# Opening the second layer's attention inside the first feed-forward's last batch, and selection logits two batches ahead

## The reference, cut to what matters

```python
xn = layernorm(x)
x = x + L0_attn(xn) + L0_ffn(xn)      # causal attention, 16 heads of 16; FFN: silu(w1 x)*(w2 x), gelu(h1 .), gelu(h2 .), w3, ternary weights 256/1024
xn = layernorm(x)
x = x + L1_attn(xn) + L1_ffn(xn)
# L1_attn: softmax(q k^T / 4 + pos_bias[h, i, j]) v, then Wout
# L1_ffn, in groups of 16 tokens, for 64 expert slots:
logits = grouped @ controller + tie
perm = logits == max(logits over the 16 tokens)
sel = perm^T grouped;  inter = relu(sel @ f1 + bias) @ f2;  out = perm inter
```

## Time and profile before

| | us |
|---|---|
| median of 3 runs | 2090.08 |
| lowest, highest | 2089.43, 2093.64 |
| the profiled execution's own time | 2090.87 |
| its span, first to last instruction | 2089.0 |
| PE busy over the span | 1777.4 (85%) |
| DVE busy | 1168.1 (56%) |
| ACT busy | 1057.0 (51%) |
| POOL busy | 984.3 (47%) |
| mean granted TensorE clock | 0.931 |

### The profile page before, as it was taken

One profiled execution on the slowest core, in us unless ns is written; L12 is line 12 of the kernel. 1 busy time (PEld: TensorE's weight loads), 2 busy tenths in 40 slices (PEclk: granted clock), 3 DMA queues, 4 the chain that ended last, 5 costly groups with the idle time before them and its releaser, 6 DMA issues. The chain is left out here.

```text
span 2089.0 us, 34151 instructions
## 1 busy us (share of the span) xinstructions
PE 1777.4 (85%) x11015; PEld 1144.5 (55%) x11015; DVE 1168.1 (56%) x2538; ACT 1057.0 (51%) x1439; POOL 984.3 (47%) x736
## 2 busy tenths in 40 slices
PE   4888898887999999999997848878878888866999
PEld 2455555544878788788785623334334334334566
DVE  5666666562243353353442348877877877926535
ACT  1555555555422232232222117877877877963542
POOL 3344444432333434334333317776776776954202
PEclk7999999997999999999998958989989989988999
DMA  3333333315411120111110173232222222107346
GB/s 109 93 102 101 97 91 101 86 47 177 143 61 33 45 78 23 55 53 43 60 43 24 34 258 87 62 77 85 61 73 89 61 71 81 32 11 289 100 150 212
DMA packets 119221, 182.52 MB, mean 87 GB/s; under 512 B 14197, under 2 KB 73077, under 8 KB 119146
## 3 DMA queue, kind: packets, MB, share of 16 engines
q1 hardware_dynamic: 109214, 170.45, 27.1%
q10 hardware_dynamic: 9296, 9.05, 1.3%
q0 software_dynamic: 640, 2.10, 0.3%
HBM read 90.72 MB, written 39.91 MB: 63 GB/s over the span
## 5 line engine op out<-in xcount | busy, mean ns | idle before, releaser
L803 POOL TENSOR_TENSOR l_prob<-l_prob,l_bias 128x1024 f32<-128x1024 f32 x192 | 452.2, 2377 | 148.4 <-ACT l_prob L918 147.6
L1202 POOL TENSOR_TENSOR f_hl<-f_full,f_hh 128x512 fp32r<-128x512 f32 x192 | 247.6, 1290 | 425.6 <-DVE f_hh L1240 271.2
L985 DVE CUSTOM_DVE_ANT_0 l_slot<-l_slot,l_bias 128x512 f32<-128x512 f32 x512 | 340.8, 716 | 52.0 <-PE l_slot L1063 51.0
L921 ACT ACTIVATE l_prob<-l_prob 128x1024 f32<-128x1024 f32 x256 | 271.1, 1071 | 0.0
L472 DVE TENSOR_REDUCE l_peak<-l_slot 128x2 f32<-128x256 f32 (+3 forms) x256 | 206.4, 822 | 108.1 <-PE l_slot L564 105.8
L1288 PE MATMUL f_ps<-f_hh,f_hi_h 128*128 128x512 f32 x1024 | 259.9, 391 | 0.8 <-ACT f_attn L1168 0.4
L1288 PE MATMUL f_ps<-f_hl,f_hi_h 128*128 128x512 f32 x1024 | 258.4, 390 | 0.0
L388 ACT ACTIVATE l_prob<-l_slot 128x1024 f32<-128x1024 f32 (+3 forms) x256 | 174.8, 706 | 101.7 <-PE l_slot L583 99.3
L1288 PEld LDWEIGHTS f_ps<-f_hh,f_hi_h 128*128 128x128 f32 x1024 | 192.3, 188 | 43.3 <-ACT f_hh L1214 2.1
L1288 PEld LDWEIGHTS f_ps<-f_hl,f_hi_h 128*128 128x128 f32 x1024 | 192.4, 188 | 39.7
L918 ACT COPY l_prob<-l_slot 128x1024 f32<-128x1024 f32 x192 | 194.8, 1014 | 36.6 <-PE l_slot L1079 35.8
(11 more groups left out here) (205 smaller groups left out, 2844.4 us busy)
## 6 DMA issues: line engine op xcount, KB each, us to landing
l_stacks<-l_parts SPq DMA_DIRECT2D x384, 128.0 KB, 2.6
attn<-l_out_sb ACTq DMA_DIRECT2D x16, 512.0 KB, 2.9
f_raw<-in_L_ffn_h_w SPq DMA_DIRECT2D x16, 512.0 KB, 3.8
f_raw<-in_L_ffn_h_w SPq DMA_DIRECT2D x32, 256.0 KB, 2.6
e_w<-in_L_ffn_f SPq DMA_DIRECT2D x32, 256.0 KB, 2.9
l_bias<-ext SPq DMA_DIRECT2D x16, 448.0 KB, 6.4
l_x_in<-in_L_attn_x SPq DMA_DIRECT2D x8, 512.0 KB, 3.9
xh<-l_xh SPq DMA_DIRECT2D x8, 512.0 KB, 2.6
```

The source lines that it names most:

```text
L803: return eng.tensor_tensor(probs(n), src, bias[:, h:h + 2, j * P:j * P + T], ALU.add)
L921: act.activation(probs(n), probs(n), ACT.Exp).then_inc(p_exp.sem, 1)
L985: ins = dve.tensor_tensor_reduce(src, src, bias[:, 4 * g + 2 * pr + a, t * P:t * P + T], 1.0, 3 * NEG, ALU.add, ALU.max, peak[:, g, a, pr, ...
L1202: pool.tensor_tensor(t.hl[layer % 2][:, o], t.full[:, n % 2], t.hh[layer % 2][:, o].bitcast(F32), ALU.subtract).then_inc(self.h_lo.sem, 1)
```

## The change

1. `biased_attention` and `layers` become generators, so that the feed-forward's block can hold work of layer 1. The tiles are laid out anew so that what is written early in layer 1 lies on tiles that are dead by then; no tile's size or type changes.
2. In the last feed-forward batch the seven pieces are rounded and compared beside h1 instead of h2. The maxima are reduced behind h1, PE turns them behind h2's third tile, and DVE makes the flag beside the fourth.
3. The branch block is gone. Each engine reads the flag inside the feed-forward block (`if_not_exact`): SP after the last pieces are issued, POOL, ACT and PE behind their last batch, DVE between its last cast and the output.
4. Behind that the opening of layer 1 follows in the same block. SP: rows, constants, weights and twelve bias heads, then the store of the last output. POOL: the power, then both halves of `stacks`. ACT: four weights, four rows. DVE: statistics and shift ahead of the output, four weight remainders behind it.
5. The wait for the last store moves from the end of the feed-forward block to SP's load of batch 1's rows.
6. In layer 1's block stay POOL's fills (key row source, now 2x512 instead of 2x4096 and broadcast, and the ones) and the last four bias heads at once.
7. In selection SP, DVE and PE run by `two_ahead`: after PE's fourth product of batch b come the transposes of b + 1 and then the logits of b + 2. DVE makes the blocks of b + 1, then logits, maximum and mask of b + 2. All eight copies are ACT's. The experts' first loads are issued after the first logits' operands of batch 1 instead of before.

The core of the diff:

```diff
+        def load_bias(sp, g):
+            for h in range(4 * g, 4 * g + 4):
+                rising = bass.AP(w["ext"].tensor, w["ext"].offset + h * 2 * T, [[1, P], [1, UW]])
+                sp.dma_start(bias[:, h], rising).then_inc(bias_in[g].sem, 16)
+
+        def open_sp(sp):
+            sp.dma_start(x_in[:], x_d[0].rearrange("(t p) d -> p t d", p=P)).then_inc(x_loaded.sem, 16)
+            for dst, src in ((power, c["c_pow"]), (ident, c["c_ident"])):
+                sp.dma_start(dst[:], src).then_inc(consts_in.sem, 16)
+            for name, ap in w["loads"]:
+                for dst, src in w["place"](name, raw[name], ap):
+                    sp.dma_start(dst, src).then_inc(w_in[name].sem, 16)
+            sp.dma_start(raw["o"], w["wo"].rearrange("(k p) n -> p k n", p=P)).then_inc(w_in["o"].sem, 16)
+            for g in range(QUADS - 1):
+                load_bias(sp, g)
+
+        def open_pool(pool):
+            pool.wait_ge(consts_in.sem, 16 * 2)
+            pool.wait_ge(eps_done.sem, 1)
+            pool.tensor_tensor(rstd[:], var_eps[:], power[:], ALU.pow).then_inc(rstd_ready.sem, 1)
+            pool.memset(stacks[:, 0].bitcast(F32), 0.0).then_inc(blank.sem, 1)
+            pool.memset(stacks[:, 1].bitcast(F32), 0.0).then_inc(blank.sem, 1)
+
+        def open_act(act):
+            for name in names + ("o",):
+                act.wait_ge(w_in[name].sem, 16)
+                act.activation({"q": wq, "k": wk, "v": wv, "o": wo}[name][:, 0], raw[name], ACT.Copy,
+                               scale=HD ** -0.5 if name == "k" else 1.0).then_inc(w_high.sem, 1)
+            act.wait_ge(shift_ready.sem, 1)
+            for t in range(TT):
+                act.activation(xn[:, t], x_in[:, t], ACT.Identity, bias=shift[:, t:t + 1],
+                               scale=rstd[:, t:t + 1]).then_inc(xn_ready.sem, 1)
+
+        def open_dve(dve):
+            dve.wait_ge(x_loaded.sem, 16)
+            for t in range(TT):
+                dve.bn_stats(stats[:, t], x_in[:, t]).then_inc(stats_done.sem, 1)
+            for t in range(TT):
+                dve.wait_ge(stats_done.sem, t + 1)
+                dve.bn_aggr(moments[:, t], stats[:, t]).then_inc(moments_done.sem, 1)
+            dve.wait_ge(moments_done.sem, TT)
+            dve.tensor_scalar(var_eps[:], moments[:, :, 1], EPS, None, ALU.add).then_inc(eps_done.sem, 1)
+            dve.wait_ge(rstd_ready.sem, 1)
+            dve.scalar_tensor_tensor(shift[:], moments[:, :, 0], -1.0, rstd[:], ALU.mult, ALU.mult)\
+               .then_inc(shift_ready.sem, 1)
+
+        def open_weights(dve):
+            for m, (name, dst) in enumerate((("q", wq), ("k", wk), ("v", wv), ("o", wo))):
+                dve.wait_ge(w_high.sem, m + 1)
+                dve.scalar_tensor_tensor(dst[:, 1], raw[name], HD ** -0.5 if name == "k" else 1.0,
+                                         dst[:, 0].bitcast(F32), ALU.mult, ALU.subtract).then_inc(w_ready.sem, 1)
+
+        opening_of = Opening()
+        opening_of.sp, opening_of.pool, opening_of.act, opening_of.dve, opening_of.weights = \
+            open_sp, open_pool, open_act, open_dve, open_weights
+        yield opening_of
...
+                        if isinstance(b, int) and b == 1:
+                            sp.wait_ge(x_stored.sem, x_stored.at(1, B - 1))
...
-                        if n in (1, 2) and opening(b):
-                            load_bias(n + 1)
...
                 sp.wait_ge(blank.sem, 3)
-                sp.dma_start(stacks[HROWS - 1:P:HROWS, 1].bitcast(F32), minus).then_inc(keyed.sem, 16)
-                for g in range(2):
-                    load_bias(g)
+                sp.dma_start(stacks[HROWS - 1:P:HROWS, 1].bitcast(F32), minus.unsqueeze(1).to_broadcast([2, PAIRS, T])).then_inc(keyed.sem, 16)
+                load_bias(sp, QUADS - 1)
...
                 pool.memset(minus, -1.0).then_inc(blank.sem, 1)
-                pool.memset(stacks[:, 1].bitcast(F32), 0.0).then_inc(blank.sem, 1)
-                pool.wait_ge(consts_in.sem, 16 * 2)
+                pool.memset(vals_sb[:], 0.0).then_inc(ones_ready.sem, 1)
+                pool.wait_ge(ones_ready.sem, 1)
+                pool.memset(vals[:, :, HD:HD + 1], 1.0).then_inc(ones_ready.sem, 1)
...
-                dve.memset(vals_sb[:], 0.0).then_inc(ones_ready.sem, 1)
-                dve.wait_ge(ones_ready.sem, 1)
-                dve.memset(vals[:, :, HD:HD + 1], 1.0).then_inc(ones_ready.sem, 1)
-                dve.memset(stacks[:, 0].bitcast(F32), 0.0).then_inc(blank.sem, 1)
...
+        if rows_ahead:
+            rows_ahead()
...
+                if beside:
+                    beside(KH + n)
...
+    def if_not_exact(eng, again):
+        eng.wait_ge(found.sem, 3)
+        with eng.If(eng.value_load(flag[0:1, 0:1], min_val=0, max_val=1) == 1):
+            eng.sem_inc(idle.sem, 1)
+            eng.wait_ge(idle.sem, 5)
+            again(eng)
...
+            load_attn(B - 1)
+            pieces(B - 1)
+            if_not_exact(sp, again_sp)
+            opening.sp(sp)
+            store(B - 1)
...
+            if_not_exact(pool, again_pool)
+            opening.pool(pool)
...
+            def table_beside(n):
+                if n == 4:
+                    table.first_copy(act)
+                if n == KH - 2:
+                    table.copies(act)
+                if KH <= n < 2 * KH:
+                    round_piece(B - 1, n + KH)
...
+            if_not_exact(act, again_act)
+            opening.act(act)
...
+            def flag_beside(n):
+                if KH <= n < 2 * KH:
+                    compare(B - 1, n + KH)
+                if n == 2 * KH - 1:
+                    dve.wait_ge(worst_done.sem, worst_done.at(1, B - 1))
+                    dve.tensor_reduce(worst_of[:], worst[:].rearrange("p a n -> p (a n)"), AX_X, ALU.max)\
+                       .then_inc(found.sem, 1)
+                if n == 2 * KH + 3:
+                    dve.wait_ge(worst_ps.sem, 1)
+                    dve.tensor_reduce(top_of[:], psum[0][0:1, 0:P], AX_X, ALU.max).then_inc(found.sem, 1)
+                    dve.wait_ge(found.sem, 2)
+                    dve.tensor_scalar(flag[:], top_of[:], 0.0, None, ALU.is_gt).then_inc(found.sem, 1)
+
+            def rows_ahead():
+                if_not_exact(dve, again_dve)
+                opening.dve(dve)
+
+            with dve.Fori(0, B - 1) as i:
+                f.dve_batch(dve, i, t, lambda n: compare(i, n) if n >= 2 * KH else None)
+            f.dve_batch(dve, B - 1, t, flag_beside, rows_ahead)
+            opening.weights(dve)
...
+                if o == 2 * KH + 2:
+                    pe.wait_ge(found.sem, 1)
+                    pe.transpose(psum[0][0:1, 0:P], worst_of[:], ident[:]).then_inc(worst_ps.sem, 1)
+
+            f.pe_batch(pe, B - 1, t, all_there, table_beside)
+            if_not_exact(pe, again_pe)
...
+def two_ahead(eng, ahead, middle, back):
+
+
+
+
+    def next_of(b, s):
+        return lambda: middle(b, s)
+
+    def second_of(b, s):
+        return lambda: ahead(b, s)
+
+    def nothing():
+        pass
+
+    ahead(0, 0)
+    middle(0, 0)
+    ahead(1, 1)
+    for s in range(2):
+        back(s, s, next_of(s + 1, (s + 1) % 2), second_of(s + 2, s))
+    with eng.Fori(1, B // 2 - 1) as i:
+        for s in range(2):
+            back(i * 2 + s, s, next_of(i * 2 + (s + 1), (s + 1) % 2), second_of(i * 2 + (s + 2), s))
+    back(B - 2, 0, next_of(B - 1, 1), nothing)
+    back(B - 1, 1, nothing, nothing)
...
+                def back(b, s):
                     for n in range(2 * TT):
-                        if n not in BY_DVE:
-                            wait(act, sel_ps, n + 1, b)
-                            act.activation(chosen(n, b), picked(n), ACT.Copy)\
-                               .then_inc(copied["act"].sem, 1)
-                skewed(act, front, nothing, back)
+                        wait(act, sel_ps, n + 1, b)
+                        act.activation(chosen(n, b), picked(n), ACT.Copy).then_inc(copied.sem, 1)
+                skewed(act, front, back)
...
+                def middle(b, s):
 
                     wait(dve, tr_ps, 1, b)
                     wait(dve, sel_ps, 2 * TT, b - 2)
-                    dve.tensor_tensor(blocks[:, s, t], tr_bank[:, t * P:(t + 1) * P:2].unsqueeze(1).to_broadcast([P, G, E]),
-                                      group[:].unsqueeze(2).to_broadcast([P, G, E]), ALU.mult)\
-                       .then_inc(blocks_ready.sem, 1)
-
-                def back(b, s, after):
                     for t in range(TT):
-                        if 2 * t in BY_DVE:
-                            wait(dve, sel_ps, 2 * t + 1, b)
-                            dve.tensor_copy(chosen(2 * t, b), picked(2 * t))\
-                               .then_inc(copied["dve"].sem, 1)
-                        if t >= TT // 2:
-                            after(2 * t - TT)
-                            after(2 * t - TT + 1)
-                skewed(dve, front, middle, back)
```

(74 more changed lines are left out.)

504 lines of the change are left out of this document (212 added, 292 removed).

## The result

The changed kernel takes 2058.25 us (median of four runs, 2055.64 to 2063.62) against 2089.76 us before (four runs): ratio 0.9853, 95% interval 0.9833 to 0.9873. Forecast were 2059.0, between 2052 and 2069. The profiled execution took 2058.57 us, span 2056.8, mean clock 0.934. PE's work is nearly unchanged, since nothing was taken off it: from part 1 of the page,

The account below looks back on a forecast made before the run. TensorE was taken as full in the last feed-forward batch, layer 1's opening as a chain, selection as a ring. Gains of 20.4 and 10.8 us, 31.2 together, off 2090.1 gave 2059 us, range 2052 to 2069.

Parts of the forecast that it names:

- Part 1: Last feed-forward batch: rounding and comparing pieces beside h1 is covered as well as beside h2; cost 0.3 us.
- Part 2: End of the feed-forward block: next block opens earlier, POOL last, PE transposing at 1196.8 instead of 1211.2; gain 14.4 us.
- rival D: PE's flag branch: its fetch waits behind bias loads in flight; slower only from some 36 us, 2100; chance 0.02.
- Part 3: Layer 1's opening to first scores: chain keeps 21 us, DVE's remainders and wait for batch 1's rows go; gain 6.0 us.
- The stall is gone: Layer 1's opening: rows of batch 1 land before DVE comes to them, removing its 4.93 us wait.
- rival C: Layer 1's opening: PE's clock stays up over the gap, saving about 5 us more, 2054; chance 0.07.
- the whole shift passes on: Layer 1 after the opening: DVE is late next, busy 11.97 of 12 us, so the opening's gain carries on fully.
- Part 4: Selection: logits two ahead shorten the period from 7.69 to 5.9 us over six periods; gain 10.8 us, bounds 0 to 11.6.
- The mask: Selection on DVE: 0.69 us instead of 1.63, since POOL's subtraction would lie beside the blocks, not the mask.
- The sum: Whole kernel: 20.4 us up to the first scores plus 10.8 in selection, 31.2 us off the median, giving 2059 us.
- A: Feed-forward block's end: branches cost DVE, ACT and POOL PE's price or more; 3.3 us less gain, 2062; chance 0.14.
- B: Selection stays a ring, mask blocked by POOL or ACT the bound; 2063, or 2070 if nothing is won; chance 0.16.

Follow-up runs that it names:

- the opening alone: The changed kernel with the selection of the kernel before: 2069.39 us against 2090.86 for the kernel before, ratio 0.9897.
- Kernel 5: The changed kernel with no bias table loaded in the feed-forward block, but all four groups in layer 1 as before: 2066.06 us in one run.
- kernel 9: The changed kernel with POOL's second fill back in layer 1, selection's constants on three semaphores and the last picks on DVE: 2055.07 us against 2061.04.

## Why the prediction was right, step by step

**Part 1**, flag work beside h1: held. From h1 of the last batch on PE shows no wait until the block's end, and the one transpose of the maxima took 0.27 us.

**Part 2**, 14.4 us; 15.37 measured. That is above the bound of 15.2 that the prediction gave for this part; by its own terms, with PE last at 1195.0, the bound should have read 15.4. POOL's second fill was last, as said. In the old trace's time its end is 1191.68 + 3.67 = 1195.35 (I had 1196.0) and the x turn 1195.86 (1196.8). Two sizes were off: the flag on DVE 1.09 us instead of the rounded 1.6, and from POOL's end to PE 0.5 us instead of 0.8. SP's issue of a bias load took 0.54 us and not 0.86, which changed nothing. One step was wrong and cost nothing: PE's branch was taken at its old price and from the last product's end. It was 2.2 us longer, for the reason of rival D, and began 1.4 us before the last product ended. Both together put PE's drain at 1191.3 + 3.67 = 1195.0, the number forecast, by chance. In the repeat of the changed kernel the branch took 6.15 us, and there the x turn was 64.28 us behind the GELU instead of 64.11.

**Part 3**, 6.0 us; 6.29 measured. The chain to the first scores took 21.0 us at clock 0.50 (first score product at 1213.15), the rows of batch 1 were issued at 1213.88, 21.69 us behind the x turn (21.7 forecast), and DVE's statistic of them began 4.45 us later (4.5), with no wait shown. The changed kernel, then the opening alone:

```profile
1213.15 0.98 PE L1093 MATMUL l_slot<-l_stacks 63*128 63x512 f32 x6
...
1213.88 0.54 SPq L875 DMA_DIRECT2D l_x_in<-x  x1
...
1218.33 0.43 DVE L990 BATCH_NORM_STATS2 l_stats<-l_x_in 128x6 f32<-128x256 f32 x1
```

```profile
1215.60 0.97 PE L1093 MATMUL l_slot<-l_stacks 63*128 63x512 f32 x6 [1.33 <-DMA l_stacks<-l_parts]
...
1217.45 0.53 SPq L875 DMA_DIRECT2D l_x_in<-x  x1
...
1222.19 0.43 DVE L990 BATCH_NORM_STATS2 l_stats<-l_x_in 128x6 f32<-128x256 f32 x1 [1.94 <-DMA l_x_in<-x]
```

"The stall is gone" was a little too much: in the eight other executions with this order of loads the statistic comes at the same distance (26.0 to 26.9 us behind the x turn), and in seven of them DVE still waits there, for 0.6 to 1.9 us. In six of these seven the clock came back to 1.00 for a part of the chain (mean 0.59 to 0.71 over the 21 us behind the x turn), and the first scores were up to 1.1 us earlier, 19.8 to 20.7 us behind the x turn. That brought nothing: the rows were issued no sooner, 21.6 to 21.7 us behind the x turn, and DVE waited for them instead. In these executions the loading of batch 1's rows sets the pace there, and not DVE or the clock, as part 3 and rival C had it. Kernel 5 shows that the bias loads had made the difference. That the whole shift passes on fits the pair (638.6 and 638.9 us from there to selection), but this stretch wanders by over 4 us; the better evidence is the 21.5 us of the opening alone. Parts 1 to 3: 21.7 by the stretches, 21.5 by the runs of the opening alone, for 20.4, both a little above the upper bound of 21.3.

**Part 4**, 10.8 us; 7.1 by the stretches, 7.5 by the runs. This is the step that was mis-sized, in two directions. The period is 5.58 us, not 5.9: PE's load had been scaled from a stretch of 8 us and came out 0.17 too high, and the 0.15 added for hand-offs didn't come: PE is never kept waiting. The six old periods, too, were 7.80 on average, not 7.69. That made 13.3, above the upper bound of 11.6. But the sum took the six periods for the whole stage. It left out that a new order of issue also changes which load is last at the start (2.0 against this one execution of before), which engine is last at the end (1.7), and through the length of PE's stand the clock of the stage behind (2.5). Rows for the first two were at hand: DVE's wait for the parity table was 3.90 us before, and that POOL's last store lies behind everything follows once ACT and PE finish earlier.

**The mask** behaved as read: 0.69 us in the steady state, where POOL's subtraction (from 1905.68) starts after it. In the first batch the mask started at 1869.98 beside a subtraction that had begun at 1868.58, and took 1.49 us. The Trainium skill ("SBUF — State Buffer", SBUF: two separate sides) calls the shared port an exclusive lock for the whole instruction; the trace agrees with that.

**The sum.** 21.7 + 7.1 - 0.3 = 28.5 us in the pair of profiles, 31.5 between the medians of the first runs, 28.0 between those of the repeat, for 31.2 forecast. The total was right partly by luck: errors of both signs met, 1.3 too little for the opening, 3.7 too much for selection, and the 3 us between the first medians and the stretches or the repeat lie within the runs' spread of 4 us to each side. Of the rivals, A didn't come (branches on DVE, ACT and POOL under 0.1 us beside full DMA engines), B didn't (PE is the bound of selection), C didn't as meant (the opening began at clock 0.50 in every execution, behind a stand of 5.1 us in this one; where the clock came back before the scores, nothing was gained), and D came as a mechanism, at 2.2 us, far under its threshold.

## What to carry to other kernels

When independent work is moved out from behind a wait, count the queue and not the wait: here the wait was worth 0.4 us and what stood behind it some 15. For a loop that becomes shorter, price its first pass, its last pass and the first instructions of the next stage by themselves; they gave back 6.2 of 13.3 us in this pair, and 5.3 us (1.9 at the start, 1.4 at the end, 2.1 of clock) returned in kernel 9 with edits of a few lines. Give a constant that only one engine reads a semaphore of its own, and let the last batch's side output be made by an engine that is idle there.

## What was not expected of the hardware

The same branch around the redo pass costs 0.05 us on POOL, 0.06 on DVE and at least 3.35 on PE. The Trainium skill ("Runtime: NRT & Kernel Launch", Instruction fetch mechanics) says that a taken branch out of the prefetched window "forces a DMA fetch of the target page". The trace agrees as far as it goes: 3.35 to 3.69 us with the DMA engines nearly idle (four executions), 4.99 to 6.15 with the last of twelve tables of 448 KB still in flight (eight). In the changed kernel the tables' traffic went on for about 2.8 us past the branch's start, and the branch was 2.2 us longer.

PE's sequencer reaches a branch while its last products are still running (1.4 us ahead here), so part of the branch's time is hidden where PE was busy up to it.

A stand of PE of up to 1.87 us ahead of apply left the clock at 1.00, and one of 3.2 us was followed by half clock for 14 to 26 products. It happened in all eight executions with that stand and cost 1.1 to 2.6 us against before (apply's products took 130.05 to 131.55 us, against 128.91 to 129.30 in the four without it).
